# A token table and row gathers in place of scattered rows in a four-layer transformer kernel, with the sort and the covariance norm moved

## The reference

```python
x = x + attn_rope(_layernorm(x))
x = x + ffn(_layernorm(x))
x = x + attn_cov(_layernorm(x))
x = x + ffn(_layernorm(x))

def ffn(x):                       # 16 heads of 8, 8 experts, top 2
    h = x + attention(layer_norm(x, ln1_w, ln1_b), w_qkv, b_qkv, w_o, b_o)
    t = layer_norm(h, ln2_w, ln2_b)
    probs = softmax(t @ w_gate)
    tw, ti = top_k(probs, 2)
    tw = tw / sum(tw)
    for e in range(8):
        we = sum(where(ti == e, tw, 0))
        out = out + we * (gelu(t @ w1[e] + b1[e]) @ w2[e] + b2[e])
    return h + out

def attn_cov(x):                  # heads of 8; q_c, k_c are centred q, k
    cov = q_c @ k_c.T / 8
    var = (sum(q_c ** 2) / 7) * (sum(k_c ** 2) / 7).T / 8
    return softmax(cov + var) @ v @ Wo.T
```

## Time and profile before

| | us |
|---|---|
| median of 3 runs | 830.07 (829.78 to 832.45) |
| profiled execution | 825.84 |
| its span | 824.0 |
| PE busy | 724.6 (88%) |
| PE weight loads busy | 547.9 |
| DVE busy | 540.3 |
| ACT busy | 535.1 |
| POOL busy | 483.1 |

### The profile page before, as it was taken

One profiled execution on the slowest core, in us unless ns is written; L12 is line 12 of the kernel. 1 busy time (PEld: TensorE's weight loads), 2 busy tenths in 40 slices (PEclk: granted clock), 3 DMA queues, 4 the chain that ended last, 5 costly groups with the idle time before them and its releaser, 6 DMA issues.

```text
span 824.0 us, 21303 instructions
## 1 busy us (share of the span) xinstructions
PE 724.6 (88%) x7166; PEld 547.9 (66%) x7166; DVE 540.3 (66%) x1370; ACT 535.1 (65%) x1264; POOL 483.1 (59%) x906
## 2 busy tenths in 40 slices
PE   1999999999999969989887998999999996999960
PEld 1765665666676559989865565666666654899950
DVE  5689999888989623112576888888888973311222
ACT  0277777787887737646546667777878873865630
POOL 6657778877754561505755665865686357060536
PEclk9789999999999979999989999999999997999985
DMA  9400000000000245667110000000000015486832
GB/s 274 144 2 3 2 4 3 3 3 3 3 4 3 69 138 155 205 182 216 54 35 14 15 18 8 3 3 3 3 4 3 3 35 162 126 231 180 256 91 70
DMA packets 57657, 56.29 MB, mean 68 GB/s; under 512 B 6856, under 2 KB 42448, under 8 KB 57552
## 3 DMA queue, kind: packets, MB, share of 16 engines
q1 hardware_dynamic: 39200, 39.13, 16.7%
q0 software_dynamic: 4096, 8.40, 3.4%
q10 hardware_dynamic: 14256, 7.41, 3.1%
HBM read 40.10 MB, written 14.29 MB: 66 GB/s over the span
## 4 chain that ended last, share of the span: by engine, by line
PE 52%; DVE 19%; POOL 14%; issue 8%; DMA 3%; ACT 2%; SPq 0%; ACTq 0%; POOLq 0%; DVEq 0%
DVE M L1110 11%; PE bankR L727 9%; PE bankE L714 9%; PE bankO L477 8%; PE bankE L450 7%; PE bankE L496 6%; PE bankR L463 4%; POOL Yg L1601 2%; POOL sorted_u L1581 2%; PE bankE L702 1%; DVE X L1343 1%; PE bankR L517 1%; POOL R L1475 1%; PE bankE L487 1%; POOL Zhl L1458 1%
## 5 line engine op out<-in xcount | busy, mean ns | idle before, releaser
L1110 DVE TENSOR_REDUCE M<-bankR 128x2 f32<-128x512 f32 x512 | 326.9, 684 | 58.8 <-PE bankR L463 56.0
L839 ACT ACTIVATE Pr<-bankE 128x512 f32<-128x512 f32 x512 | 275.9, 594 | 101.8 <-PE bankE L450 101.2
L463 PE MATMUL bankR<-KQ 32*128 32x256 f32 x1024 | 168.7, 336 | 13.5 <-DVE M L1110 5.5
L477 PE MATMUL bankO<-Pr,Vx 128*32 128x256 f32 x2048 | 139.2, 389 | 2.3 <-ACT OT L833 1.3
L450 PE MATMUL bankE<-KQ 32*128 32x256 f32 x1024 | 139.7, 331 | 1.3 <-ACT Pr L839 1.1
L450 PEld LDWEIGHTS bankE<-KQ 32*128 32x128 f32 x1024 | 85.4, 186 | 78.0 <-issue 46.2
L1332 DVE COPY Yb<-bankR 128x128 f32<-128x128 f32 x92 | 26.8, 291 | 156.3 <-PE bankR L727 150.2
L463 PEld LDWEIGHTS bankR<-KQ 32*128 32x128 f32 x1024 | 104.0, 189 | 31.1 <-DVE M L1110 25.8
L952 ACT ACTIVATE G<-bankE,W 128x128 f32<-128x128 f32 x368 | 101.0, 378 | 20.3 <-PE bankE L714 19.6
L1581 POOL DMA_INDIRECT sorted_u<-U,SLOT x64 | 62.3, 974 | 82.4 <-DVE past L1312 43.1
L1601 POOL DMA_INDIRECT Yg<-sorted_y,SLOT x64 | 62.1, 970 | 81.5 <-DVE Yb L1332 57.8
(11 more groups left out here) (169 smaller groups left out, 1089.3 us busy)
## 6 DMA issues: line engine op xcount, KB each, us to landing
W<-in_w1b SPq DMA_DIRECT2D x92, 258.0 KB, 3.2
sorted_y<-Yb ACTq DMA_DIRECT2D x92, 64.0 KB
XT<-sorted_u SPq DMA_DIRECT2D x20, 256.0 KB, 2.9
sorted_u<-Yg SPq DMA_DIRECT2D x2, 1472.0 KB, 9.9
KQ<-MT SPq DMA_DIRECT2D x128, 4.0 KB
X<-in_x SPq DMA_DIRECT2D x8, 128.0 KB, 7.2
sorted_u<-U,SLOT POOLq DMA_INDIRECT x64
Yg<-sorted_y,SLOT POOLq DMA_INDIRECT x64, 2.6
```

The costliest lines, as they stand in the source:

```text
L463: k = mm(dve_bank("raw", layer, b, h)[:, z * T:z * T + T], QT[rows, kb, g, z * P:z * P + P], KT[rows, kb, g, :], start=True, stop=True)
L477: k = mm(bankO[SL * j:SL * j + SL, cols], Vx[:, b % VB, kc, HG * g + j, :], Pr[:, g % 2, j, kc, :], start=(g % 2 == 0 and kc == 0), stop=( ...
L839: nc.scalar.activation(Pr[:, (h // HG) % 2, h % HG], act_bank("S", layer, b, h).rearrange("p (k q) -> p k q", k=TT), ACT.Exp, scale=EXP_SC ...
L1110: v.tensor_reduce(M[:, b % 2, :, h], dve_bank("raw", layer, b, h).rearrange("p (t k) -> p t k", t=TT), AX.X, ALU.max, negate=True).then_in ...
```

## The change

Rows are no longer scattered. SP writes U of every sequence unsorted to u_rows in DRAM (keep_rows) as soon as it is normalised. A token table TOK says for each place of each tile which token stands there; POOL gathers each tile of 128 rows by one indirect DMA (fetch_rows), 23 per half where 16 scatters and 6 loads were. The tiles of a half have buffers of their own: eight in XT, the rest in the part of KQ that the last sequence's keys and queries have left. sorted_u and its zeroing go.

The table is made by a product of two masks. split_places gives each row's tile and its row in the tile, and a mask of the tile times the token (in_tile, 16 groups of 24 columns); mark_rows gives a mask of the row in the tile (in_row, 16 groups of 128 columns, in Zhl and R). find_owners on PE multiplies them in 16 matmuls of 128 by 24, and copy_owners on DVE casts the result to TOK.

The sort of half 0 moves: do_rank part 1 goes to the end of PE's step of b6, and the DVE functions count_tiles, place_rows and name_experts go to the step in which a is b7, with the new functions behind them. For half 1 the new functions stand at tiles 6, 7 and 8.

In the covariance layer combine() and norm_in() of b4 to b7 move on DVE from behind the fifth pair of row maxima to behind the second, zT of b3 to b7 moves on PE to the end of the step of p, and POOL's four gathers of the next sequence, which stood singly between the stackings, stand now two ahead of stack_k and two behind norm(). PE also turns the second group of tiles of a half behind three hidden() instead of ahead of them.

```diff
+        def x_tile(q, j):
+            if q % (NGRP // 2) < NXG:
+                return XT[:, q % (NGRP // 2), j, :]
+            at = (q % (NGRP // 2) - NXG) * XG + j
+            return as32(KQ[:, at // 8, 0].rearrange("p g x -> p (g x)")[:, (at % 8) * D:(at % 8) * D + D])
...
-            return LAYERS[q[0]] != "cov"
+            return q[0] != 2 or q[1] >= FILL
...
-            sp.wait_ge(zero_set, 1)
-            for half in range(2):
-                sp.dma_start(sorted_u[half].rearrange("(i p) d -> p i d", p=P),
-                             Yg[:, 0:1, :].broadcast_to([P, NTL, D])).then_inc(zeroed, 16)
...
+            def keep_rows(layer, b):
+                if LAYERS[layer] == "ffn":
+                    need(sp, u_ready, layer, b, 6)
+                    half = b // HB
+                    if layer == 3:
+                        need(sp, x_turned, 0, (half + 1) * NGRP // 2 - 1)
+                    sp.dma_start(u_rows[half][(b % HB) * T:(b % HB) * T + T, :].rearrange("(t p) d -> p t d", p=P),
+                                 U[:, b]).then_inc(u_out[half], 16)
...
+                for b in range(NB - DRAIN, NB):
+                    keep_rows(2 * ph + 1, b)
+                for at in range(NW, NAT):
+                    load_w(ph, at)
...
-                if ranking(a):
-                    do_rank(a[0] // 2, 0, 1)
...
+                if last_step(a):
+                    find_owners(a[0] // 2, 0)
...
+            def find_owners(ph, half):
+                ring_r.take(pe, ("owners", ph, half))
+                bank = dve_bank("owners", ph, half)
+                for c in range(2):
+                    need(pe, sorted_, ph, half, 19 + c)
+                    for n in range(GROUPS // 2):
+                        g = c * GROUPS // 2 + n
+                        k = mm(bank[:, 0:NTC], in_row(c)[:, n * P:n * P + P],
+                               in_tile[:, g * NTC:g * NTC + NTC], start=g == 0, stop=g == GROUPS - 1)
+                    k.then_inc(owned.sem, 1)
...
                     turn_x(ph, half * NGRP // 2)
-                    turn_x(ph, half * NGRP // 2 + 1)
                     for at in range(half * NTL, half * NTL + LEAD):
                         hidden(ph, at)
+                    turn_x(ph, half * NGRP // 2 + 1)
...
+                if last_step(a):
+                    count_tiles(a[0] // 2, 0)
+                    place_rows(a[0] // 2, 0)
+                    name_experts(a[0] // 2, 0)
+                    split_places(a[0] // 2, 0)
...
+                if late(p):
+                    combine(0, p[1])
+                    norm_in(*p)
...
+                if last_step(a):
+                    mark_rows(a[0] // 2, 0)
...
+            def split_places(ph, half):
+                def done(x):
+                    need(dve, sorted_, ph, half, x)
+                v.tensor_scalar(tile_of[:], place[:], 1.0 / P, (P - 1) / (2.0 * P), ALU.mult,
+                                ALU.subtract).then_inc(sorted_.sem, 1)
...
+                v.scalar_tensor_tensor(row_of[:], tile_of[:], -float(P), place[:], ALU.mult, ALU.add).then_inc(sorted_.sem, 1)
+                at = in_tile.rearrange("p (g i) -> p g i", g=GROUPS)
+                tt(at, tile_col.unsqueeze(1).broadcast_to([P, GROUPS, NTC]),
+                   tile_of[:].unsqueeze(2).broadcast_to([P, GROUPS, NTC]), ALU.is_equal).then_inc(sorted_.sem, 1)
+                done(17)
+                tt(at, as32(at), token.unsqueeze(2).broadcast_to([P, GROUPS, NTC]), ALU.mult).then_inc(sorted_.sem, 1)
...
+            def mark_rows(ph, half):
+                need(dve, zT, 2 * ph + 1, NB - 1)
+                need(dve, sorted_, ph, half, 18)
+                for c in range(2):
+                    own = slice(c * GROUPS // 2, (c + 1) * GROUPS // 2)
+                    tt(in_row(c).rearrange("p (g r) -> p g r", g=GROUPS // 2),
+                       row_no.unsqueeze(1).broadcast_to([P, GROUPS // 2, P]),
+                       row_of[:, own].unsqueeze(2).broadcast_to([P, GROUPS // 2, P]),
+                       ALU.is_equal).then_inc(sorted_.sem, 1)
...
+            def fetch_rows(ph, half, q):
                 layer = 2 * ph + 1
-                if 0 in part:
-                    need(pool, sorted_, ph, half, 10)
-                    need(pool, u_ready, layer, HB * half + HB - 1, 6)
-                    if ph:
-                        need(pool, x_turned, ph - 1, (half + 1) * NGRP // 2 - 1)
-                    else:
-                        pool.wait_ge(zeroed, 2 * 16)
-                for n in part:
+                for j in range(GROUP[half * NGRP // 2 + q][1]):
+                    at = q * XG + j
+                    if at == 0:
+                        need(pool, sorted_, ph, half)
+                        pool.wait_ge(u_out[half], 16 * HB * (ph + 1))
                     if half:
-                        need(pool, evacuated, ph, PACE_AT + 4 * n // 5)
-                    elif n in PACE:
-                        need(pool, exped, layer, *PACE[n])
-                    b, t = divmod(half * HB * TT + n // 2, TT)
-                    g.indirect_dma_start(sorted_u[half][:, :],
-                                         bass.IndirectOffsetOnAxis(ap=SLOT[:, half, n:n + 1], axis=0),
-                                         U[:, b, t, :], None).then_inc(scattered[half], 16)
+                        need(pool, x_turned, ph, q)
+                    elif ph:
+                        need(pool, x_turned, ph - 1, NGRP // 2 + q)
+                    if not half and q == 0 and j == 2:
+                        need(pool, exped, layer, NB - 1)
+                    if not half and q == 1 and j:
+                        need(pool, (outT, onT, wo)[j - 1], layer, NB - 1)
+                    if not half and q == NXG and j == 0:
+                        need(pool, scores, layer, NB - 1)
+                        need(pool, raw, layer, NB - 1)
+                    if half:
+                        need(pool, evacuated, ph, 9 + 4 * at // 5)
+                    g.indirect_dma_start(x_tile(q, j), None, u_rows[half][:, :],
+                                         bass.IndirectOffsetOnAxis(ap=TOK[:, half, at:at + 1], axis=0)).then_inc(
+                        x_in[q], 16)
...
+                if filling:
+                    gather(0, p[1] + 1, range(0, 1))
                 if fetched:
-                    gather(0, p[1] + 1, range(0, 1))
+                    gather(0, p[1] + 1, range(0, 2))
...
-                    gather(0, p[1] + 1, range(3, 4))
+                    gather(0, p[1] + 1, range(2, 4))
...
-                    if s == STEPS - DRAIN - 2:
-                        scatter(ph, 0, range(EARLY))
+                        gather(0, 1)
                     if s == STEPS - DRAIN - 1:
-                        scatter(ph, 0, range(EARLY, GROUPS))
+                        fetch_rows(ph, 0, 0)
+                        fetch_rows(ph, 0, 1)
+                    if s == STEPS - DRAIN:
+                        fetch_rows(ph, 0, 2)
                     if s == STEPS - 1:
-                        scatter(ph, 1)
-            for b in range(NB):
+                        for q in range(NXG + 1, NGRP // 2):
+                            fetch_rows(ph, 0, q)
+                        for q in range(NGRP // 2 - 1):
+                            fetch_rows(ph, 1, q)
...
```

126 lines of the change are left out of this document (69 added, 57 removed).

## The result

The changed kernel takes 840.55 us (838.52 to 843.44, four runs) beside 831.26 for the kernel before (829.78 to 834.68, four runs): a ratio of 1.0121, with an interval of 1.0086 to 1.0157. The forecast was 825.4, faster. Timed twice more (e1, e9), the changed kernel gave 1.0090 (1.0057 to 1.0123) and 1.0077 (1.0050 to 1.0104): about 1% slower. Every ratio here leaves out executions that took over 1.5% longer than the fastest of the same kernel.

What follows compares the result with a forecast made beforehand. PE is hardly idle inside attention and mixture, so only seams and covariance steps give time: -5.6 + 5.2 - 5.8 + 6.2 - 4.5 - 0.2 = -4.7, median 830.07 to 825.4, range 813 to 832.

Steps and rivals of the forecast that it cites:

- The covariance steps: Covariance layer: cycle 18.75 instead of 18.12, +2.7 together; -2.9 in the step ahead; sum -0.2, bounds -9 to +5.
- what the gathers give, the later hsq takes: Covariance step: POOL's time saved on gathers is lost to a later hsq; Zhl ready at 16.0, before 15.9.
- The slower rival: Covariance steps: late hsq makes zT wait, clock falls; 2.5 more per step, +12.5 instead of -0.2, 838; chance 0.12.
- The step of b7: End of attention: sort, masks and find_owners come in; +2.6 per phase, +5.2, bounds +1.5 to +4 per phase.
- The table in the mixture: Tile 8: find_owners and its mask waits cost 3.1 per phase, 1.85 of it work; +6.2.
- The halves' seam: Between the mixture's halves: PE's weight waits of 1.86 and 0.77 go; -3.7 and -0.8, together -4.5.
- The step of b6: Attention: the sort leaves DVE, step shrinks from 15.84 to about 13.0; -2.8 per phase, -5.6.
- The mixture's start: Seam from attention: row wait of 6.22 goes, wait of about 3 for U of b7 comes; -2.9 per phase, -5.8.
- The two ends: Start to the first product, and phase 1's third group to the span's end: no change, 0.
- the faster rival: Covariance chain and POOL's queue both slack: 810.7, or 814.7 with the first alone; chance 0.27.

Runs made afterwards that it cites:

- e1: The changed kernel timed again, unaltered: ratio to the kernel before 1.0090 (1.0057 to 1.0123).
- e9: The changed kernel timed once more, unaltered: median 839.29 us, ratio to the kernel before 1.0077 (1.0050 to 1.0104).
- e2: The changed kernel with sum, zT and gathers of the covariance steps back as before: median 835.2 us, ratio to the kernel before 1.0041.
- e4: The changed kernel with only zT back in the next covariance step, the sum still early: ratio to the kernel before 1.0097.
- e13: The changed kernel with rank products and sort back in the step of b6, masks around the division: 1.0107 to the kernel before, from two executions.
- e15: The changed kernel with covariance steps as before, float16 masks, weights of tiles 7 to 9 first, e13's edit, find_owners at tile 9: 825.16 us, ratio 0.9938.
- e5 to e7: The changed kernel with, one each: float16 masks and table; mixture masks a tile earlier; one mask pair per set there. All 885 to 891 us, another chip.
- e16: As e15, with U of b7's turn, gate, ranks and sort one tile later in the mixture, find_owners at tile 10: 820.65 us, ratio 0.9881.
- e5: The changed kernel with masks and token table of find_owners in float16 instead of fp32r: 885 to 891 us on a chip where before took 844.47.
- e14: The changed kernel with the covariance sum in two parts, the second behind the third maxima and hsq: ratio to the kernel before 1.0119.
- e5 to e8: The runs of e5 to e7 and the changed kernel with the third group's gathers behind b7's second norm (891.49): 885 to 891 us, before 844.47.

## Why the prediction was wrong

It was not one term. Every added piece was priced by its work, and the clock was charged twice only (behind the wait for U, and given back at the seam).

- **The covariance steps** (-0.2 forecast, +4.1 measured with the stretch ahead of b0's product, 3.0 of it the edit's): the step that failed is "what the gathers give, the later hsq takes", with a cycle of 18.75. The chain over POOL, on which the forecast's cycle is built, doesn't hold the step: Zhl is written by 484.40 and zT asks for it at 486.01. But the sum moved ahead of hsq was moved ahead of the third maxima too, and I did not ask who waits for those: PE, 2.56 and 2.22 per step, at half clock behind it. The cycles were 19.9, 19.7 and 18.9. The slower rival named the place wrongly (zT) and charged 2.5 per step, where 1.8, 1.3 and 0.3 were lost; that its 838 lies near the 840.6 measured is luck. The trace, e2 and e4 show the cause.
- **The step of b7** (+2.6 each forecast, +4.4 and +3.9): the matmuls were priced at 1.85 and took 2.03 to 2.09, and of the waits for the masks one of 0.49 came, in phase 1. (By its own figures, 10.2 less 7.3, the forecast should have charged 2.9.) What was left out are the rank products, moved from the head of the step of b6 to its end, thus into this step (276.92 to 277.76, 0.84), a wait of 0.99 for KQ in phase 0, and the low clock behind find_owners (windows above, e13, e15).
- **The table in the mixture** (+3.1, measured +4.4 each): waits of 0.95 and about 0.4 were charged (the second mask 1.3 behind the first, less the first set's work) and one of 0.59 came. The rest is the clock (e5 to e7).
- **The halves' seam** (-3.7 and -0.8, measured -1.9 and +0.4): the waits for weights went as forecast. The turn of the second group, which the change puts behind three hidden() calls, was in the diff and in no term here: 1.40 and 0.87 of waiting for its copy, and 0.44 more for the first group's. No run puts that turn back.
- **The step of b6** (-2.8 each, measured -2.2): right in mechanism; PE's own work (12.6 busy and a wait of 0.64) fills the step 0.6 sooner than forecast.
- **The mixture's start** (-2.9 each, measured -3.1 and -3.4): right, with the wait of 3 for U of b7 and its clock fall, and without in some executions (15.2 instead of 16.7).
- **The two ends** (0, measured 1.4 and 2.2): the first is chance. Of the second 3.0 belong to the change, cause open.

Clock and waits together account for the sign. With most of the clock falls of the table and the wait for U gone it is 1.2% faster than before (e16): 10 us, between the 4.7 of the forecast and the 15 to 19 of the faster rival, and for other reasons than either gave.

## What to carry to other kernels

When work is moved on an engine, list everything that it is moved past, and for each of these who waits; a chain that still closes on time says nothing of the buffers that come free later. A wait or a run of small matmuls is worth its own length only where PE stays at 2.4 GHz behind it: look at the windows behind each new gap, and price the products that follow at 1.2 GHz as the dear case. And one profile of a kernel like this can be 6 us off its next (spans of 836.7 and 830.3 here), so compare stretches between instructions that both kernels have.

## What was new of the hardware

- Eight matmuls with 128 columns of weights and 24 of data took 1.03 us in fp32r (changed kernel) and 0.35 in float16 (e5).
- The granted clock fell from 2.4 to 1.2 GHz behind 2.0 us of such fp32r matmuls with PE busy without a gap (e13, one execution), and not behind 0.5 us of the float16 ones in the same place (e15, e16, four places).
- Nearly equal waits of PE (5.1 and 5.0 us in four steps) went with a clock of 0.98 before and of 0.87 in e14, where they lie in the middle of the step.
- The same stretch of a program kept its clock in one execution and lost it in the next: behind the unaltered find_owners in the mixture 14 of 20 places show the fall, at 1.6 us each.
- A ratio of two programs depends on the chip: the changed kernel was 0.8 to 1.2% slower than the kernel before in three comparisons, and four near variants of it 4.8 to 5.6% on a chip where the kernel before took 1.5% longer (e5 to e8).
